# A 16-unit transformer loop on one core: the scan's place on VectorE and the late constants' place in a step

## What is computed

```python
y = silu(layernorm(h, ln1_w, ln1_b))
y = sconv(y, phazor, last_conv)          # a causal convolution with p**t, per channel, complex p
h = h + y * sc_lin
y = layernorm(h, ln2_w, ln2_b)
y = silu(y @ W1.T + b1) @ W2.T + b2      # 64 -> 256 -> 64
h = h + y
```

## Time and profile before

| what | value |
|---|---|
| median of 3 runs | 272.15 us (272.02 to 272.39) |
| the profiled execution | 272.17 us |
| its span | 270.4 us |
| busy: TensorE matmul, weight load | 206.9 us (77%), 148.5 us (55%) |
| busy: VectorE, ScalarE, GpSimd | 198.8 us (74%), 116.0 us (43%), 83.4 us (31%) |
| mean granted TensorE clock | 0.921 of full speed |
| input and set-up | to about 44 us |
| steps 2 to 17 of the main loop | about 44 to 153 us |
| first output and memory stage, to the end | about 153 to 270 us |

### The profile page before, as it was taken

How to read it: one execution, slowest core, us unless ns; L and a number is a source line. 1 busy time by engine, 2 the same in 40 slices (tenths; PEclk the granted TensorE clock), 3 DMA queues, 4 the chain that set the end, 5 groups by cost and what they waited for, 6 DMA issues and landing times.

```text
span 270.4 us, 3479 instructions
## 1 busy us (share of the span) xinstructions
PE 206.9 (77%) x1106; PEld 148.5 (55%) x1106; DVE 198.8 (74%) x590; ACT 116.0 (43%) x283; POOL 83.4 (31%) x119
## 2 busy tenths in 40 slices
PE   2964865875778788888888875899999999759630
PEld 2864863764567565667776751565555555323200
DVE  7897999996267866666777415677777975889994
ACT  3422111342244354445745444444324326869440
POOL 2603332324122222223332322222122120019872
PEclk9979599597779999999999997999999999999875
DMA  6999800000000000000000000000000000002436
GB/s 195 336 393 397 263 2 0 0 4 0 0 0 2 0 0 2 1 0 4 0 0 2 0 0 0 0 2 0 1 1 2 0 0 0 0 4 78 156 137 251
DMA packets 6868, 15.10 MB, mean 56 GB/s; under 512 B 897, under 2 KB 1761, under 8 KB 6338
## 3 DMA queue, kind: packets, MB, share of 16 engines
q1 hardware_dynamic: 6850, 14.88, 15.5%
HBM read 10.68 MB, written 4.19 MB: 55 GB/s over the span
## 4 chain that ended last, share of the span: by engine, by line
PE 43%; DVE 32%; ACT 12%; issue 6%; POOL 5%; POOLq 0%; DVEq 0%; ACTq 0%
PE bank L1157 13%; PE bank L1092 6%; PE bank L1133 6%; PE bank L1106 5%; DVE BN L710 4%; ACT HD L461 3%; POOL RS L320 3%; PE bank L1062 3%; PE bank L1080 2%; DVE SS L729 2%; ACT Z L454 2%; PE bank L1144 2%; DVE Z L743 2%; DVE XT L961 2%; DVE X L967 2%
## 5 line engine op out<-in xcount | busy, mean ns | idle before, releaser
L320 POOL TENSOR_TENSOR RS<-SS,nhalf 128x4 f32<-128x4 f32 x36 | 37.7, 1047 | 87.6 <-DVE SS L729 87.6
L1157 PE MATMUL bank<-SW_,Y 128*128 128x384 f32 x128 | 43.9, 485 | 0.0
L729 DVE TENSOR_REDUCE SS<-SQ 128x4 f32<-128x260 f32 x36 | 15.2, 421 | 26.8 <-ACT SQ L440 26.6
L1106 PE MATMUL bank<-ffst,HD 128*128 128x128 f32 x256 | 33.3, 286 | 0.7 <-ACT HD L461 0.7
L1157 PEld LDWEIGHTS bank<-SW_,Y 128*128 128x128 f32 x128 | 23.9, 190 | 17.0 <-issue 4.2
L1106 PEld LDWEIGHTS bank<-ffst,HD 128*128 128x128 f32 x256 | 32.1, 204 | 1.3 <-ACT HD L461 1.0
L461 ACT ACTIVATE HD<-bank,ffst 128x512 f32<-128x512 f32 x32 | 20.3, 684 | 16.8 <-PE bank L1092 16.8
L1092 PE MATMUL bank<-Z,w1st 64*128 64x256 f32 x128 | 19.3, 422 | 7.6 <-ACT Z L454 7.6
L440 ACT ACTIVATE SQ<-bank 128x256 f32<-128x256 f32 x36 | 13.7, 382 | 23.4 <-DVE bank L722 15.9
L1037 PE MATMUL bank<-wcc,XT 128*128 128x128 f32 x128 | 21.0, 341 | 3.3 <-DMA XT<-in_xT 2.5
L1037 PEld LDWEIGHTS bank<-wcc,XT 128*128 128x128 f32 x128 | 20.6, 256 | 3.7 <-DMA XT<-in_xT 3.7
(11 more groups left out here) (222 smaller groups left out, 387.9 us busy)
## 6 DMA issues: line engine op xcount, KB each, us to landing
XT<-in_xT SPq DMA_DIRECT2D x4, 1024.0 KB, 13.7
X<-in_x SPq DMA_DIRECT2D x4, 1024.0 KB, 15.5
out<-X SPq DMA_DIRECT2D x8, 512.0 KB, 2.8
w1r<-in_w1d SPq DMA_DIRECT2D x1, 514.0 KB, 9.2
lt<-in_late SPq DMA_DIRECT2D x1, 385.5 KB, 14.8
c<-in_c SPq DMA_DIRECT2D x1, 301.5 KB, 10.1
w2r<-in_w2t SPq DMA_DIRECT2D x1, 256.0 KB, 13.7
SW_<-in_wu SPq DMA_DIRECT2D x1, 256.0 KB
```

What stands on the lines that cost most here:

```text
L320: pool.tensor_tensor(RS[:, g, :], SS[:, g, :], nhalf[:, :], ALU.pow).then_inc(done, 1)
L729: dve.tensor_reduce(SS[:, g, :], SQ[:, g, :, :], AX.X, ALU.add).then_inc(done, 1)
L1106: last = pe.matmul(HK[g][:, j * P:(j + 1) * P], HD[:, u % 2, a, at:at + P], ffst[:, L, a * P:(a + 1) * P], start=False, stop=True, skip_gr ...
L1157: last = pe.matmul(SBK[t % 4][:, 0:SW], XNT[:, t % 4, c * P:(c + 1) * P], SW_[:, c, :], start=False, stop=(c == VC - 1))
```

## The change

VectorE runs the scan of unit s - 1 ahead of the second scale of unit s - 2. TensorE runs the late piece's matmuls between hidden and mix_in, and ScalarE reads them between silu2 and the square of unit s - 1. No operation is added or taken away.

```diff
@@ scalar, step
                 if ffn:
                     silu2(s - 2, 0)
                     silu2(s - 2, 1)
+                if 0 <= s - LATE0 < LATES:
+                    setup_late(s - LATE0)
                 if 0 <= s - 1 < UNITS:
                     square(s - 1, (a1, s), sq2)
@@ scalar, main loop
                 step(s)
-                if 0 <= s - LATE0 < LATES:
-                    setup_late(s - LATE0)
@@ vector, step
                 if s < GROUPS:
                     sum_squares(s, sq1, ss1)
+                if conv:
+                    scan(s - 1)
                 if 0 <= s - 2 < UNITS:
                     scale(s - 2, rs2, z2)
                 if conv:
-                    scan(s - 1)
                     demodulate(s - 1)
```

## The result

The changed kernel took 281.62 us (median of 4, 281.46 to 285.92) against 272.27 us before (median of 4). The ratio is 1.036, interval 1.031 to 1.041: slower by 9.4 us. The ratio is one of means; it leaves out executions more than 1.5% above the fastest of their kernel, here the one of 285.92 us, and takes in two more, of 282.73 and 283.86 us. The forecast was 284.8 us in a range of 280.8 to 289.0.

The account below looks back on a forecast made before the run. No engine bounds the kernel; time goes from hand to hand, and the moved scan joins the steady loop. Terms 1.0 - 0.4 + 0 + 2.3 + 2.6 + 1.65 + 5.45 = +12.6 on 272.17 gave 284.8 us, range 280.8 to 289.0.

Parts of the forecast that it names:

- The loop of the steady step: Main-loop steps without late constants: from turn2 through silu1, modulate, scan and scale, 6.78 us instead of 5.69.
- The faster rival: The scale starts right behind the scan's start, so the scan costs the path nothing: about -3, 269 us; chance 0.05.
- Steps 11 to 15: Steady main-loop steps: the scan enters the loop and costs 1.09 us in each, +5.45 us.
- The rival in which the clock falls again and again: TensorE idle time brings its clock down in steps 11 to 15 or 8 steps: 291 to 295 us; chance 0.13.
- Steps 8 to 10: Main-loop steps with late matmuls: 7.85 us with both parts against 7.30, a loss of 0.55 each, +1.65 us.
- The late move alone: Late work in the middle without the scan's move: late steps 6.76 us against 7.30, a gain of 0.54 each.
- Step 6: Eight late matmuls and the score rows, with nothing covering them or the scan: 10.06 us against 7.74, +2.3.
- Step 7: 7.18 us at full clock, +0.7, plus 1.9 for a clock fall after step 6's idle time: together +2.6.
- Step 4: Late matmul and bias row at the lower clock: 11.3 to 12.4 us, taken as 11.7 against 12.14, -0.4.
- Later stages: Input, output and memory stages keep their order and only shift; difference 0.

Follow-up runs that it names:

- short_scan: The changed kernel with the scan's recurrence left out, VectorE multiplying instead: 272.32 us, ratio 1.003 to the kernel before.
- scan_only: The kernel before with only the scan moved ahead of the second scale, late pieces left at the step's end: 282.51 us, ratio 1.040.
- scan_tail: The kernel before with the scan ahead of the scale only from step 12 on, where no late piece is left: 275.65 us, ratio 1.015.
- again: The changed kernel, unaltered, run once more for another profile: 283.11 us, ratio 1.041 to the kernel before.
- late_again: Second run of the changed kernel with VectorE's old order, so only the late pieces are moved: 267.45 us, ratio 0.982 to the kernel before.
- spread: `late_only` with VectorE's bias row ahead of step 4's sum of squares and six score-row operations spread over steps 6 to 11: 262.06 us, ratio 0.964.
- fill: The changed kernel with extra TensorE matmuls ending each step from 4 to 15, four each, thirteen in step 6: 279.47 us, ratio 1.031.
- late_only: The changed kernel with VectorE's old order, so only the late pieces are moved: 263.50 us, ratio 0.971 to the kernel before.
- before: The kernel without the change, in its first profile: the profiled execution took 272.17 us.
- before_again: The kernel without the change, run again for a second profile: its profiled execution took 272.18 us.

## Why the prediction was right, and where it was off

The measured time is in the range, 0.8 us above its lower end, and its reason is the one given: the scan is in the loop. The sum of +12.6 was too large against the +9.4 of the medians, and that its terms came as near as that is in part luck, as the steps show. By its own steps:

- **The loop of the steady step.** "New loop from turn2 ... 6.78" measured 6.75. The pitch behind a scan, bounded by 0 and 1.22 and taken as 1.15, measured 1.14. `short_scan` shows it from the other side. The faster rival needed a hold under 0.1 us and is out.
- **Steps 11 to 15**, forecast +5.45: 5.3 are the loop (five times 6.75 - 5.69), and 2.9 more are two falls of the clock. The prediction said "at 1.00 from step 8", and that was wrong. The rival in which the clock falls again and again had the right mechanism with the wrong count: one step of the five in `scan_only` and `scan_tail`, two in `again`, none with the idle time filled. The single 1.3 us ahead of step 7 that left the clock at 1.00 was read as evidence for safety; one idle gap that did no harm says little about the same gap in step after step. The Trainium skill (page "TensorE: Matmul & The Clock Gate", section "HAM oscillation") says that a loop whose every pass leaves PE idle for long enough loses the clock on every pass. This trace agrees in kind and not in measure: here 1.28 and 0.47 us of idle time a step, shorter than the waits in the page's example, were enough, and the clock fell in 1 or 2 of the five steady steps unless their idle time was filled or shortened.
- **Steps 8 to 10**, forecast +1.65, measured +1.1. The term that was too large is the late matmul's 1.07, read from piece 4 and charged three times. In `again` these steps are 7.80, 7.60 and 7.61. Piece 4 adds 1.05 to the 6.75, as charged; pieces 5 and 6, two matmuls of 256 columns each, add 0.85. In step 9 hidden starts at 109.53, the late piece 0.97 behind it and mix_in 0.95 behind that, where hidden to mix_in alone is 1.07:

```profile
110.50 1.02 PE L1028 MATMUL bank<-KB,c 64*128 64x256 f32 x4
111.45 1.16 PE L1064 MATMUL bank<-cvst,U 128*128 128x128 f32 x8
```

- **The late move alone**, worked out as 0.54 a step, gives (21.91 - 19.59)/3 = 0.77 in `late_again`. One part of the rest is the late matmul, as above. The other is the prediction's "sum of squares + 1.69": that had ScalarE's square waiting for silu2, and with mix_in later the square waits for nothing but mix_in, so the sum of squares stands 1.61 behind it (98.69 - 97.08 in step 8). The total gain, 3.5 in the expectation, was 8.1 and 5.7 in the two sets.
- **Step 6**, 10.06 forecast, 9.94 measured; "Nothing covers them or the scan" held, until `spread` gave the score rows a cover.
- **Step 7**, +2.6 forecast, +3.2 measured. `fill` splits it: 7.10 without the fall (7.18 was forecast), so the fall cost 2.5 where I took 1.9. The fall goes with the idle time at the end of step 6. Over the twelve profiles the clock fell in step 7 behind 3.47 us (`again` and the first profile), 2.96 (`short_scan`) and 2.56 (`scan_only`); behind 2.23 in `late_only` and not in `late_again`; and in none of the six with 1.31 or less, `before` and `fill` (0.57) among them.
- **Step 4**, -0.4 forecast, -3.3 measured. This is the largest miss in the sum. The step charged the late matmul "at the lower clock (twice 1.07)" and a penalty of 1.34 or more, as if the fall of the earlier trace rows belonged to the step. It does not: the same code gave 12.14, 10.74 and 9.14 us. It goes with whether the clock has fallen in step 3 already. In six of the twelve profiles step 3 was at 1.00 and step 4 at 0.64 to 0.84; in the other six step 3 was at 0.63 to 0.80 and step 4 at 0.89 to 1.00. A fall in step 3 is nearly free where VectorE is the bound: in the old order the step took 8.52 or 8.53 us at either clock. All four profiles with the scan ahead from the start had the fall in step 3, two of seven with the old order did; `short_scan` had it in step 4. Whether the scan's place moves it is not tested. The errors of step 4 and of steps 11 to 15 have opposite signs, and so the sum of the profiled executions, +11.0, was nearer to +12.6 than its terms were. That is luck.
- **Later stages**, forecast "only shift": -1.7 in `again`, +0.1 in `fill`. That too is one fall of the clock more or less: in the twelve profiles this stretch took 115.2 us in the three where the clock fell twice in it, and 116.4 to 117.9 in the nine where it fell three or four times.

## What to carry to other kernels

In a software pipeline of in-order engines, find the closed loop of one steady step and ask of each moved instruction whether it enters that loop: the scan cost 1.06 us a step (6.75 against 5.69) as soon as the loop ran through it, and nothing while it stood one place behind. Work that has no deadline belongs where an engine waits for another anyway, found by the idle time ahead of an instruction; moved there, late matmuls and score rows took 3.7% off. Where the clock of TensorE falls is a property of the execution as much as of the kernel: compare stretches at equal clock before reading a difference of 1 to 3 us as an effect of the code.

## What the runs showed of the hardware that was not expected

- An independent VectorE operation starts 1.14 us after a scan of 514 elements starts (the scan shows 1.23). Behind a product of the same size that shows 0.69, it starts after 0.62.
- Idle gaps of 1.28 and 0.47 us ahead of turn2 and hidden, repeated every 6.75 us, brought TensorE's clock down in one or two of five steps per execution, at a price of 1.3 to 1.6 us each (`scan_only`, `scan_tail`, `again`). With 0.9 us of extra matmuls in each step (`fill`), it fell in none of them, and no steady step was longer than 6.75.
- A fall of the clock in step 3, where VectorE was the bound, left that step at 8.52 us (`scan_tail`, clock 0.80) as without it (`before_again`, clock 1.00), and step 4 then took 9.14 us instead of 10.74.
- Two executions of the kernel before that agree to 0.01 us (272.17, 272.18) had steps 4 and 5 split differently by 1.4 us. Equal totals don't mean equal timelines.
